# A mixture-of-experts kernel behind cross attention: the first list of tiles takes those of the first three blocks first, and the outputs are put together from an earlier slot, five in six slots

## What is computed

```python
expert_weights, q = _router(x, proj_w, anchors, routing_temp)   # softmax over the best TOP_K = 2 of 6
h = jax.nn.gelu(jnp.einsum('btd,edh->bteh', x, w1))             # (6, 512, 256)
out = jnp.einsum('bteh,ehd,bte->btd', h, w2, expert_weights)    # (6, 256, 512)
...
x = x + _L0_xattn_ref(_layernorm(x, axis=-1), ctx_1024, ctx_1024, mask_Bx1x1xS2_ik0, L0_xattn_W_out)
x = x + _L0_ffn_ref(_layernorm(x, axis=-1), L0_ffn_proj_w, L0_ffn_anchors, L0_ffn_routing_temp, L0_ffn_w1, L0_ffn_w2)
```

## Time and profile before

| | |
|---|---|
| median of 3 runs | 650.73 us (648.66 to 651.44) |
| profiled execution | 647.7 us, its span 645.0 us |
| PE busy | 564.1 us, 87% of the span |
| DVE, ACT, POOL busy | 423.5, 343.3, 300.1 us |
| mean granted clock of TensorE | 0.953 of full speed |
| transferred | 122.07 MB, mean 189 GB/s |

### The profile page before, as it was taken

How to read it: one execution, slowest core, us unless ns; L and a number is a source line. 1 busy time by engine, 2 the same in 40 slices (tenths; PEclk the granted TensorE clock), 3 DMA queues, 4 the chain that set the end, 5 groups by cost and what they waited for, 6 DMA issues and landing times.

```text
span 645.0 us, 14215 instructions
## 1 busy us (share of the span) xinstructions
PE 564.1 (87%) x4472; PEld 413.7 (64%) x4472; DVE 423.5 (66%) x895; ACT 343.3 (53%) x664; POOL 300.1 (47%) x434
## 2 busy tenths in 40 slices
PE   5678899999989899788879799998999999999950
PEld 3564355556556555444456788887999999888840
DVE  4667777667687867656989555576853357566653
ACT  3638875677758555565646364343345545444420
POOL 5434765656538665664758140404000056544443
PEclk9769999999999999999979699999999999999985
DMA  5321122222322338273447364658577789999986
GB/s 165 100 57 59 52 96 87 81 100 99 99 71 94 125 107 311 99 262 118 176 155 254 104 220 154 239 201 308 182 232 228 219 274 366 400 406 406 383 296 188
DMA packets 60274, 122.07 MB, mean 189 GB/s; under 512 B 7718, under 2 KB 10790, under 8 KB 60204
## 3 DMA queue, kind: packets, MB, share of 16 engines
q1 hardware_dynamic: 49964, 87.61, 40.2%
q0 software_dynamic: 10240, 33.56, 14.5%
HBM read 67.93 MB, written 53.22 MB: 188 GB/s over the span
## 4 chain that ended last, share of the span: by engine, by line
PE 60%; DVE 11%; DMA 11%; issue 8%; ACT 6%; POOL 2%; SPq 1%; POOLq 0%; DVEq 0%; ACTq 0%
DMA y_d<-ysb 10%; PE ps L1672 5%; PE ps L1523 4%; PE ps L1567 4%; PE ps L1544 4%; PE ps L1752 4%; PE ps L1754 4%; PE ps L1753 4%; PE ps L1778 3%; PE ps L1780 3%; PE ps L1779 3%; PE ps L1738 3%; PE ps L1568 3%; PE ps L1569 3%; PE ps L1697 3%
## 5 line engine op out<-in xcount | busy, mean ns | idle before, releaser
L798 POOL DMA_INDIRECT yg<-y_d,y_row x64 | 65.6, 1025 | 127.5 <-DMA y_d<-ysb 81.6
L728 POOL DMA_INDIRECT xs_d<-x,to_row x64 | 65.8, 1028 | 73.1 <-DVE to_row L1174 38.4
L919 ACT ACTIVATE prob<-ps 128x512 f32<-128x512 f32 x128 | 65.9, 601 | 60.5 <-PE ps L1547 60.5
L1092 DVE TENSOR_REDUCE nmax<-ps 128x4 f32<-128x512 f32 x128 | 79.5, 684 | 22.5 <-PE ps L1523 22.5
L1752 PE MATMUL ps<-w1H,xgH 128*128 x276 | 84.4, 306 | 5.6 <-DVE xgL L1407 5.0
L1407 DVE TENSOR_TENSOR xgL<-ps,xgH 128x512 fp32r<-128x512 f32 x69 | 47.5, 689 | 58.1 <-ACT xgH L1001 57.8
L1754 PE MATMUL ps<-w1L,xgH 128*128 x276 | 78.3, 284 | 0.0
L1753 PE MATMUL ps<-w1H,xgL 128*128 x276 | 78.2, 283 | 0.0
L758 POOL TENSOR_TENSOR atT<-less,raw 128x512 f32<-128x512 f32 x32 | 40.8, 1274 | 45.1 <-issue 39.0
L1778 PE MATMUL ps<-w2H,hH 128*128 x138 | 60.2, 436 | 0.8 <-DVE ysb L1420 0.8
L1021 ACT ACTIVATE ysb<-ps 128x512 f32<-128x512 f32 x43 | 25.7, 599 | 62.9 <-DMA y_d<-ysb 39.3
(11 more groups left out here) (214 smaller groups left out, 1268.9 us busy)
## 6 DMA issues: line engine op xcount, KB each, us to landing
xg<-xs_d SPq DMA_DIRECT2D x69, 256.0 KB, 3.7
y_d<-ysb SPq DMA_DIRECT2D x69, 256.0 KB, 3.2
xin<-in_x SPq DMA_DIRECT2D x32, 256.0 KB, 2.8
x<-in_x SPq DMA_DIRECT2D x32, 256.0 KB, 3.1
x_d<-x SPq DMA_DIRECT2D x32, 256.0 KB, 2.1
x2t<-x_d SPq DMA_DIRECT2D x32, 256.0 KB, 4.8
out_x<-x2t SPq DMA_DIRECT2D x32, 256.0 KB, 6.1
w1L<-in_L_ffn_w SPq DMA_DIRECT2D x6, 512.0 KB, 6.6
```

The source lines that it names most:

```text
L919: nc.scalar.activation(prob[v % 2][:, h, :], ps[:, B_SC + h, :], ACT.Exp, scale=scale).then_inc(exp_done, 1)
L1092: nc.vector.tensor_reduce(nmax[:, n % 2, :, g * hpg + h], ps[:, token_bank(h), :].rearrange("p (t k) -> p t k", t=4), axis=AX.X, op=ALU.ma ...
```

## The change

`TILES_OF` of blocks 0 to 2 becomes T1 + 5 = 32. So that this holds, the first list no longer takes the filled tiles expert by expert: it has two parts. The first holds, for every expert, those tiles that blocks 0 to 2 need (`some[:, 0]`, the lesser of `whole`, the tiles filled by four blocks, and `soon`, the tiles that three blocks begin), the second the others. If the list's 27 places don't reach, `taken` says how many of each were taken, and the second list begins with what blocks 0 to 2 still lack. That makes one class more (CLASSES 6 for 5) and eight stretches of rows for each expert instead of six (PLACES).

`put_slot(c)` becomes 41 + c + c//5 for c up to 23, and stays 70 to 73 for c = 24 to 27. Outputs 28 to 31 stay behind the loop.

```diff
-    TILES_OF = [most_tiles(max(n + 1, NB1)) for n in range(nblk)]
-    CLASSES = nblk - NB1 + 1
+    TILES_OF = [T1 + EXPERTS - 1 if n + 1 < NB1 else most_tiles(n + 1) for n in range(nblk)]
+    CLASSES = nblk - NB1 + 2
+    PLACES = CLASSES + 2
...
         def put_slot(c):
 
-            s = TILES_OF[0] + 9 + c
-            return s if s < SLOTS and TILES_OF[c // 4] < tiles else None
+            w = TILES_OF[0] + 9 + c + c // 5
+            if c // 4 >= nblk - 2:
+                w = TILES_OF[c // 4] + 9 + c % 4
+            return w if w < SLOTS and TILES_OF[c // 4] < tiles else None
...
                 rounded(cnt[:, 0, :], -HALF, whole[:])
-                tabled(nc.vector.tensor_tensor(nbef[:, 0, :, :], whole[:].unsqueeze(1).to_broadcast([P, EXPERTS, EXPERTS]),
-                                               tri[:], ALU.mult))
-                tabled(nc.vector.tensor_reduce(first[:, 0, :], nbef[:, 0, :, :], axis=AX.X, op=ALU.add))
+                tabled(nc.vector.tensor_tensor(cnt[:, 1, :], used[:, NB1 - 1, :], used[:, 0, :], ALU.subtract))
+                rounded(cnt[:, 1, :], HALF, soon[:])
+
+                tabled(nc.vector.tensor_tensor(some[:, 0, :], whole[:], soon[:], ALU.min))
+                tabled(nc.vector.tensor_tensor(some[:, 1, :], whole[:], some[:, 0, :], ALU.subtract))
+                tabled(nc.vector.tensor_tensor(nbef[:, 0:2, :, :], some[:].unsqueeze(2).to_broadcast([P, 2, EXPERTS, EXPERTS]),
+                                               tri[:].unsqueeze(1).to_broadcast([P, 2, EXPERTS, EXPERTS]), ALU.mult))
+                tabled(nc.vector.tensor_reduce(first[:, 0:2, :], nbef[:, 0:2, :, :], axis=AX.X, op=ALU.add))
+                tabled(nc.vector.tensor_reduce(nsoon[:], some[:, 0, :], axis=AX.X, op=ALU.add))
+                tabled(nc.vector.tensor_scalar(first[:, 1, :], first[:, 1, :], nsoon[:], None, ALU.add))
...
-                tabled(nc.vector.tensor_copy(zero_row1[:], zero_row[:, 0, :]))
-                list_of(1, NB1)
-                tabled(nc.vector.tensor_scalar(ntil[:, 0, :], first[:, 0, :], -1.0, float(T1), ALU.mult, ALU.add))
-                tabled(nc.vector.tensor_scalar(ntil[:, 0, :], ntil[:, 0, :], 0.0, None, ALU.max))
-                tabled(nc.vector.tensor_tensor(ntil[:, 0, :], ntil[:, 0, :], whole[:], ALU.min))
+                tabled(nc.vector.tensor_tensor(zero_row[:, 1, :], some[:, 0, :], first[:, 1, :], ALU.subtract))
+                tabled(nc.vector.scalar_tensor_tensor(zero_row[:, 1, :], zero_row[:, 1, :], float(P), used[:, 0, :], ALU.mult, ALU.add))
+                tabled(nc.vector.tensor_copy(zero_row1[:], zero_row[:, 0:2, :]))
+                list_of(2, NB1)
+                tabled(nc.vector.tensor_scalar(taken[:], first[:, 0:2, :], -1.0, float(T1), ALU.mult, ALU.add))
+                tabled(nc.vector.tensor_scalar(taken[:], taken[:], 0.0, None, ALU.max))
+                tabled(nc.vector.tensor_tensor(taken[:], taken[:], some[:], ALU.min))
+                tabled(nc.vector.tensor_tensor(ntil[:, 0, :], taken[:, 0, :], taken[:, 1, :], ALU.add))
+                tabled(nc.vector.tensor_tensor(ntil[:, 1, :], ntil[:, 0, :], soon[:], ALU.max))
...
-                    each = [P, 2 * 4, EXPERTS * (CLASSES + 1)]
+                    each = [P, 2 * 4, EXPERTS * PLACES]
```

More of the change, by code:

```diff
@@ L257, in xattn_moe @@
         lst = sb("lst", [P, 2])
[L258 to L262, removed]
+        zero_row1 = sb("zero_row1", [P, 2, EXPERTS])
+        soon = sb("soon", [P, EXPERTS])
+        some = sb("some", [P, 2, EXPERTS])
+        taken = sb("taken", [P, 2, EXPERTS])
+        nsoon = sb("nsoon", [P, 1])
+        bound = sb("bound", [P, EXPERTS, PLACES])
+        moveby = sb("moveby", [P, EXPERTS, PLACES])
+        change = sb("change", [P, EXPERTS * PLACES])
+        within = sb("within", [P, 2 * 4, EXPERTS * PLACES])
         moved = sb("moved", [P, 2 * 4])
@@ L1257, in first_list @@
                 tabled(nc.vector.scalar_tensor_tensor(zero_row[:, 0, :], first[:, 0, :], -float(P), used[:, 0, :], ALU.mult, ALU.add))
-                tabled(nc.vector.tensor_copy(zero_row1[:], zero_row[:, 0, :]))
-                list_of(1, NB1)
-                tabled(nc.vector.tensor_scalar(ntil[:, 0, :], first[:, 0, :], -1.0, float(T1), ALU.mult, ALU.add))
-                tabled(nc.vector.tensor_scalar(ntil[:, 0, :], ntil[:, 0, :], 0.0, None, ALU.max))
-                tabled(nc.vector.tensor_tensor(ntil[:, 0, :], ntil[:, 0, :], whole[:], ALU.min))
+                tabled(nc.vector.tensor_tensor(zero_row[:, 1, :], some[:, 0, :], first[:, 1, :], ALU.subtract))
[7 more added lines that the diff above has]
+                tabled(nc.vector.tensor_tensor(ntil[:, 1, :], ntil[:, 0, :], soon[:], ALU.max))
             def tiles_of_classes():
-                classes = [P, CLASSES, EXPERTS]
+                n = CLASSES - 1
                 dve.wait_ge(used_done, nblk)
-                tabled(nc.vector.tensor_tensor(cnt[:], used[:, NB1:nblk + 1, :], used[:, 0:1, :].to_broadcast(classes), ALU.subtract))
-                rounded(cnt[:], HALF, ntil[:, 1:CLASSES + 1, :])
+                tabled(nc.vector.tensor_tensor(cnt[:, 0:n, :], used[:, NB1:nblk + 1, :],
+                                               used[:, 0:1, :].to_broadcast([P, n, EXPERTS]), ALU.subtract))
+                rounded(cnt[:, 0:n, :], HALF, ntil[:, 2:CLASSES + 1, :])
                 tabled(nc.vector.tensor_tensor(nbef[:], ntil[:].unsqueeze(2).to_broadcast([P, CLASSES + 1, EXPERTS, EXPERTS]),
@@ L1285, in rows_to_tiles @@
             def rows_to_tiles():
-                n = EXPERTS * (CLASSES + 1)
-                by_expert = [x.rearrange("p c e -> p e c") for x in (ntil[:, 0:CLASSES, :], zero_row[:])]
+                n = EXPERTS * PLACES
+                ahead, starts, zeros1, zeros2 = [x.rearrange("p c e -> p e c") for x in (
+                    taken[:, 0:1, :], ntil[:, 0:CLASSES, :], zero_row1[:], zero_row[:])]
                 tabled(nc.vector.tensor_copy(bound[:, :, 0:1], used[:, 0, :].unsqueeze(2)))
-                tabled(nc.vector.scalar_tensor_tensor(bound[:, :, 1:], by_expert[0], float(P),
+                tabled(nc.vector.scalar_tensor_tensor(bound[:, :, 1:2], ahead, float(P), used[:, 0, :].unsqueeze(2), ALU.mult, ALU.add))
+                tabled(nc.vector.scalar_tensor_tensor(bound[:, :, 2:], starts, float(P),
                                                       used[:, 0, :].unsqueeze(2).to_broadcast([P, EXPERTS, CLASSES]),
                                                       ALU.mult, ALU.add))
-                tabled(nc.vector.tensor_scalar(moveby[:, :, 0:1], zero_row1[:].unsqueeze(2), -1.0, None, ALU.mult))
-                tabled(nc.vector.tensor_scalar(moveby[:, :, 1:], by_expert[1], -1.0, float(T1 * P), ALU.mult, ALU.add))
+                tabled(nc.vector.tensor_scalar(moveby[:, :, 0:2], zeros1, -1.0, None, ALU.mult))
+                tabled(nc.vector.tensor_scalar(moveby[:, :, 2:], zeros2, -1.0, float(T1 * P), ALU.mult, ALU.add))
                 flat = moveby[:].rearrange("p e c -> p (e c)")
```

## The result

The change takes 643.64 us (median of 4 runs, 640.77 to 646.41) against 651.05 us for the kernel before in the same comparison: ratio 0.9897, 95% interval 0.9861 to 0.9933. The forecast was 4.1 us faster, 0.9937. By the medians alone the three differences are 7.4, 5.7 and 4.1 us. The profiled execution took 643.1 us with a span of 640.3 us, 4.7 us shorter than the one before; that one was a short execution for its kernel (647.7 against medians of 648 to 651), so two profiles show less than the first medians. Medians here are over all executions, ratios over the fast ones, those at most 1.5% above the fastest of their kernel.

What follows compares the result with a forecast made beforehand. Transfers bound the expert stage in slots 51 to 66, PE before that; VectorE's chain bound the first list. Gains of 6.7 us minus a 2.6 us loss gave 4.1 us off 650.73, so 646.6 us; range 643.0 to 651.5.

Steps and rivals of the forecast that it cites:

- A's own range: Whole kernel: the forecast's sum of gain and loss holds, 645 to 648.5 us; chance 0.46.
- rival C: First list: the twelve added DVE operations are covered, so -6.7 us, 644.0 us; chance 0.12.
- The stage is bound by the sum of transfers from slot 51 to 66: Expert stage: six 256 KB transfers a slot at 406 GB/s take 3.87 us; before that PE binds.
- Gain 5.8 us up to slot 70: Expert stage, slots 57 to 70: thirteen slots at PE's pace take 45.07 us against 50.86.
- Gain 0.5 and 0.4 behind slot 70: First up matmul in slot 70 waits 0.5 us less for xgL; last ysb copy 0.4 less for a store.
- Sum of the gain, 6.7 us: Output schedule: the gains of 5.8, 0.5 and 0.4 us together.
- Loss 2.6 us: First list, attention stage: twelve added DVE operations delay `raw` and `newton` without cover, 2.6 us.
- B: After `newton`: the clock drops for a while, eleven matmuls cost 2.2 us more, 648.8 us; chance 0.17.
- E: After `newton`: the clock stays low about twice as long, 9.5 us more, 656.1 us; chance 0.08.
- The signs: Transposes 3.47 us apart to slot 70, stores under 6 us, `newton` 2.6 us later, PE's wait 3.7 us.
- No cost for the wider tables in the expert stage: Slots 24 to 31: wider row operations add 0.3 us a slot, against DVE's 0.27 us wait: a tie.
- Rival F: Expert stage: outputs don't come earlier or slots still take 3.9 us, only the loss stays, 653.3 us; chance 0.04.

Runs made afterwards that it cites:

- tables alone: The change's lists with outputs back on the old schedule, slots 46 to 73, run twice: 648.63 us (ratio 0.9997) and 650.03 us (1.0026).
- twelve and twenty-four operations: The kernel before with 12 or 24 small DVE operations added at the first list: 649.76 us (ratio 1.0016) and 653.37 us (1.0075).
- list operations moved: The change with nine list operations moved, 643.79 us; also five of full_tiles, 642.21 us; also outputs in four of five slots, 640.36 us.
- half residuals: The change with residuals 16 to 31 loaded by half, 256 of 512 columns: 640.34 us, ratio 0.9872.

## Why the prediction came out as it did

The time fell on the side forecast, and by somewhat more than the sum: 5.7 us over three comparisons for 4.1. The 643.64 us lie 0.6 us inside the lower end of the range, outside A's own range (645 to 648.5) and next to rival C's 644.0. The gain came about as forecast; what was wrong is the size of the loss, of which about 1 us of 2.6 arrived. So the surplus goes back to this one term as far as the runs tell, and the nearness to C's number in the first comparison is in part chance: the other two differ by 5.7 and 4.1 us in the medians.

- **"The stage is bound by the sum of transfers from slot 51 to 66": shown.** The same outputs five slots earlier at six units a slot lose 2.8 to 5.3 us from slot 50 to 60, before anything else comes in; at 5.33, 5.2 and 4.9 units all but at most four of the twenty slots from 50 on take 3.60 us or less.
- **Gain 5.8 us up to slot 70.** The change's profiles give 5.1, 2.4 and 3.1 us against the one profile before, but that one was the shortest of its schedule. Slots 50 to 70 took 75.1 to 77.4 us in the five profiles with outputs at 46+c (before, tables alone twice, twelve and twenty-four operations), 76.2 in the mean, and 69.2 to 72.7 us in the five with outputs in five of six slots (the change three times, the list operations moved twice), 70.8 in the mean. That is 5.4 us, near the 5.8. A load of 99% of what 406 GB/s carry breaks single slots, in every profile of the change slot 57 and in two of them slot 56. "At most 1.2 us in a row, half of what the buffers took" was too kind.
- **Gain 0.5 and 0.4 behind slot 70:** 1.1 to 1.6 us from the transposes of tile 68 to the end, for 0.9. The last copy's wait stayed (2.73 us), the rest of the way got shorter. Over the same five and five profiles it is 1.5 us.
- **Sum of the gain, 6.7 us:** the change against the tables alone, 0.9912 against 1.0011, is 6.4 us in the timed runs, and within the two groups that have both it is 5.1 and 6.8. The change's profiles against the one before give 4 to 6.2 us, five against five 6.9.
- **Loss 2.6 us: the term that was mis-sized.** DVE's delay is what I worked out, 2.5 us at `newton`, and PE's wait 3.66 for 3.7. What arrives in the time is about 1 us: 0.8 by the tables alone, 1.0 by twelve operations in the old kernel. I took "there is no cover" from the chain of one profile. The chain carries the delay, but PE's low-clock stretches behind `newton` and `sel` move with it: in profiles with the twelve operations they come to 3.4 to 10.2 us between 270 and 345 us, against 6.8 in the profile before, and where a stretch is saved some of the 2.5 us comes back. The profiles show it best from `newton` on, to the first up matmul: 41.6 us in the three with 3.4 us at the low clock right behind `newton`, 42.5 to 42.6 in the three with 3.4 us behind `sel` (the change's first is one), 44.2 to 44.4 in the three with both places, 10.2 us; before, with 6.8 us behind `sel`, 43.5, and in the three with list operations moved, again with 6.8 behind `sel`, 43.3 to 43.5. So where the clock was the same the way behind `newton` was as long whatever `newton`'s delay, and the differences go with the clock. That the clock gives back the difference is also read from nine profiles of kernels with these twelve operations (from `whole` to the first up matmul 51.8 to 52.9 us in six, with 3.4 us at the low clock, 54.0 to 54.5 in the three with 10.2); no experiment held the clock fixed, and there is one profile of the kernel before, so it is argued for the median.
- **Rivals B, C and E.** B (a low clock behind the new gap) and C (covered) were single executions of the same kernel and not two fates of it; the median lies between them. E's price did not come: where the clock was low in both places, 10.2 us in all, the way from `newton` to the first up matmul took 2.7 us longer than with 3.4 us right behind `newton`, not 9.5.
- **The signs.** `newton` came 2.52 us later and PE waited 3.66 us, as named. ScalarE's waits ahead of the last one did not go (14 to 16 of them from 520 us on, 20.1 to 31.0 us), and in the one profile of the change that has the landings, its third, the stores of `ysb` took 4.4 to 7.0 us between 560 and 605 us, median 5.7. That the expert stage starts no later than before (357.46 for 357.42 us) was named as the sign of a wrong step, and it is the loss that was wrong; part of it is the earlier start of the stretch, which is chance (`cnt` at 304.05 us here, at 303.47 and 307.14 in the two other profiles of the change).
- **No cost for the wider tables in the expert stage: right.** From tile 15's transposes to tile 24's two of the change's profiles took 36.0 and 34.8 us, before 35.6; the first took 37.5 with the low clock at 447 to 450 us. The three wide operations take 0.55 us for 0.45, as worked out, and slots 26 to 39 took 44.8 us against 45.0.
- **Rival F.** The change carries 378 to 394 GB/s in the window of 38 us, and the gain came. The Trainium skill (DMA: Bandwidth & Descriptors, "Where 436 GB/s comes from") has about 358 GB/s; the estimate by it, 3.90 us for 5.33 units, would have left nothing of the 3.91 us a slot to gain, and the profiles at 5.33 and six units a slot do not agree with it.

## What to carry to other kernels

Where a stage is bound by transfers for part of its slots, count them per slot in units of one size and spread them until the load is under the rate that the trace shows; at 99% of it single slots still broke here, at 91% (half residuals) none did. An earlier start without that room gained nothing. A delay on the chain of waits is not yet time: read what lies behind it, above all the stretches in which PE runs at its low clock, in more than one profile, before it goes into a sum at its full size. And a version that only its profile shows to be better (636.4 against 639.8 us here) can be the same in the median.

## What was not expected of the hardware

- PE's low-clock stretches differ from execution to execution of the same lists: 3.4 and 10.2 us before 345 us in two profiles with the same waits of 3.64 and 3.62 us. They go with 2.6 us in the time to the expert stage.
- At 5.33 transfers of 256 KB a slot the landing of a store still makes ScalarE wait 20 to 31 us in all from 520 us on, and it costs PE 1 to 4 us from slot 50 to 70; with six a slot in slots 51 to 66 the waits are 35 to 42 us, and it costs PE 6 to 8 us.
